# Expert outputs written in token order by indirect transfers, and small reorderings on GpSimd, ScalarE and VectorE in the attention layers of a two-layer decoder

## The reference, cut to what matters

```python
x = x + _L0_attn_ref(_layernorm(x), ...)          # 16 heads of 8
x = x + _L0_xattn_ref(_layernorm(x), ctx, ctx, ...)  # 16 heads of 8
x = x + _L0_ffn_ref(_layernorm(x), ...)           # 8 experts, top 2, F=512
x = x + _L1_attn_ref(_layernorm(x), ...)          # 16 heads of 64, rotary positions
x = x + _L1_xattn_ref(_layernorm(x), ctx, ctx, mask)
x = x + _L1_ffn_ref(_layernorm(x), ...)           # fake-quantised gated part
...
# _L0_ffn_ref
logits = jnp.einsum('bth,eh->bte', x, router_w) + router_b
topv, topi = jax.lax.top_k(logits, TOP_K)
gates = jax.nn.softmax(topv, axis=-1)
# per expert e: w = sum(gates * (topi == e)); y = (silu(x gw) * (x uw)) dw; acc + y * w
```

## Time and profile before

| | us |
|---|---|
| median of 3 runs | 1352.48 |
| lowest and highest run | 1347.32 to 1356.64 |
| profiled execution, its own time | 1356.87 |
| its span in the trace | 1355.1 |
| busy in the span: PE, DVE, POOL, ACT | 1055.9, 892.3, 548.8, 553.0 |
| granted TensorE clock, mean | 0.84 of full |

### The profile page before, as it was taken

One profiled execution on the slowest core, in us unless ns is written; L12 is line 12 of the kernel. 1 busy time (PEld: TensorE's weight loads), 2 busy tenths in 40 slices (PEclk: granted clock), 3 DMA queues, 4 the chain that ended last, 5 costly groups with the idle time before them and its releaser, 6 DMA issues. The chain is left out here.

```text
span 1355.1 us, 39532 instructions
## 1 busy us (share of the span) xinstructions
PE 1055.9 (78%) x14827; PEld 849.9 (63%) x14828; DVE 892.3 (66%) x2134; ACT 553.0 (41%) x877; POOL 548.8 (41%) x686
## 2 busy tenths in 40 slices
PE   2889895888967389999993899999999997462353
PEld 1466563555646289999992778788788786341012
DVE  2577663678762663444444689889889885546777
ACT  1456452555631015666651344444444443111343
POOL 3132313334402023333314878888888864203000
PEclk9799895899975559999996899999999999555555
DMA  3000001000024001111112000000000000111002
GB/s 83 1 2 0 1 1 32 17 9 15 2 84 166 8 14 42 47 48 46 46 36 84 16 13 10 12 10 10 12 10 11 10 0 19 46 48 31 0 0 62
DMA packets 33367, 37.54 MB, mean 28 GB/s; under 512 B 6344, under 2 KB 26507, under 8 KB 32908
## 3 DMA queue, kind: packets, MB, share of 16 engines
q1 hardware_dynamic: 28942, 27.64, 6.7%
q0 software_dynamic: 4352, 8.92, 2.5%
HBM read 27.63 MB, written 8.91 MB: 27 GB/s over the span
## 5 line engine op out<-in xcount | busy, mean ns | idle before, releaser
L1167 POOL DMA_INDIRECT e_x<-xn_rows,e_where x72 | 68.3, 948 | 205.4 <-DVE e_where L1148 119.1
L1137 DVE COPY e_y<-e_Y_ps 128x128 f32<-128x128 f32 x72 | 21.0, 292 | 110.9 <-PE e_Y_ps L1104 110.9
L1094 PE MATMUL e_G_ps<-e_xT,e_gate_here 128*128 128x128 f32 x576 | 78.3, 280 | 0.5 <-ACT e_up_here L1057 0.5
L1094 PE MATMUL e_U_ps<-e_xT,e_up_here 128*128 128x128 f32 x576 | 77.8, 279 | 0.0
L1104 PE MATMUL e_Y_ps<-m_down_w,e_hT 128*128 x576 | 76.3, 275 | 1.2 <-issue 1.0
L1303 POOL TENSOR_TENSOR a_RQ<-a_PQ 128x256 f32<-128x256 f32 x64 | 46.3, 724 | 75.4 <-DVE a_PQ L1648 75.4
L1572 ACT ACTIVATE a_OT<-a_VQ_ps 128x512 f32<-128x512 f32 x64 | 38.2, 597 | 89.0 <-PE a_VQ_ps L1468 89.0
L1056 ACT ACTIVATE e_gate_here<-m_gate_w 128x512 f32 x72 | 45.4, 630 | 70.3 <-PEq L85 44.9
L1094 PEld LDWEIGHTS e_G_ps<-e_xT,e_gate_here 128*128 128x128 f32 x576 | 72.0, 196 | 0.7 <-ACT e_up_here L1057 0.7
L1094 PEld LDWEIGHTS e_U_ps<-e_xT,e_up_here 128*128 128x128 f32 x576 | 71.8, 196 | 0.0
L1104 PEld LDWEIGHTS e_Y_ps<-m_down_w,e_hT 128*128 128x128 f32 x576 | 70.3, 192 | 0.9 <-issue 0.9
(11 more groups left out here) (302 smaller groups left out, 2885.5 us busy)
## 6 DMA issues: line engine op xcount, KB each, us to landing
slot_out<-e_y SPq DMA_DIRECT2D x72, 64.0 KB
x_ctxT<-in_ctxT SPq DMA_DIRECT2D x16, 256.0 KB
m_gate_w<-in_L_ffn_gate_w SPq DMA_DIRECT2D x1, 2048.0 KB
m_up_w<-in_L_ffn_up_w SPq DMA_DIRECT2D x1, 2048.0 KB
m_down_w<-in_L_ffn_down_w SPq DMA_DIRECT2D x1, 2048.0 KB
xn_rows<-r_xn SPq DMA_DIRECT2D x8, 256.0 KB
x_ctxK<-in_ctxK SPq DMA_DIRECT2D x8, 256.0 KB
out_x<-q_y SPq DMA_DIRECT2D x8, 256.0 KB, 2.2
```

The costliest lines, as they stand in the source:

```text
L1094: mm = nc.tensor.matmul(out[:, c * P:(c + 1) * P], w[:, p, c * P:(c + 1) * P], xT[:, p, :], start=True, stop=True)
L1167: nc.gpsimd.indirect_dma_start(out=x[:, j, :], out_offset=None, in_=k.xn_rows, in_offset=bass.IndirectOffsetOnAxis(ap=where[:, j, :], axis ...
```

## The change

Four things are changed. (1) The expert phase no longer stores its tiles to `slot_out`. The plan phase numbers the pairs 1 + choice*4096 + token, keeps these numbers per row as `targets` (0 for padding), and derives `tokens` from them by four more small instructions on DVE. POOL then writes each tile's rows by an indirect transfer to the row of `chosen_out` that `targets` names; padding rows all go to row 0. So that two of these transfers are never under way at once, POOL waits for the one before to have landed. `y` has four buffers, and the store of tile t stands on POOL behind the gather of tile t+8. (2) The wide attention reads both choices of a block by two plain transfers from SP, 128 KB each; POOL's gathers and ACT's index copies are gone. (3) In the wide attention combine moves from items 1 and 2 to items 0 and 1, statistics from item 3 to item 2, and power, centre and normalise from item 0 to item 3 of the step before. (4) In the narrow attention spread_k stands ahead of power.

```diff
@narrow_attention_phase, POOL
             def step(blk, p, prev, nxt):
+                if nxt:
+                    spread_k(blk + 1, 1 - p)
                 if nxt == 2:
                     power(blk + 2)
-                if nxt:
-                    spread_k(blk + 1, 1 - p)
                 add_bias(blk)
@plan_phase, DVE
-            nc.vector.tensor_copy(tokens[:], token_ps[:, 0:NT])
+            chained(nc.vector.tensor_copy(token_f[:], token_ps[:, 0:NT]))
+            nc.vector.tensor_copy(targets[:], token_f[:])
+            chained(ts(second[:], token_f[:], float(NU * P + 1), float(-NU * P), ALU.is_ge, ALU.mult))
+            chained(tt(token_f[:], token_f[:], second[:], ALU.add))
+            nc.vector.tensor_scalar(tokens[:], token_f[:], -1.0, 0.0, ALU.add, ALU.max)
@expert_phase, SP: the whole block is removed
-                wait_here(sp, y_ready, t + 1, passed)
-                sp.dma_start(k.slot_out[bass.ds(t * P, P), :], y[:, p, :]).then_inc(stored[p], 16)
@expert_phase, DVE
-            def output(t, p):
+            def output(t, j):
+                s = j % YB
+                if later(t, YB):
+                    dve.wait_ge(stored[s], (t // YB) * 16)
+                nc.vector.tensor_copy(target[:, s, :], targets[:, bass.ds(t, 1)])
                 dve.wait_ge(y_done, t + 1)
-                if later(t, 2):
-                    dve.wait_ge(stored[p], (t // 2) * 16)
-                nc.vector.tensor_copy(y[:, p, :], Y_ps[p][:, 0:C]).then_inc(y_ready, 1)
+                nc.vector.tensor_copy(y[:, s, :], Y_ps[j % 2][:, 0:C]).then_inc(y_ready, 1)
@expert_phase, POOL
+            def scatter(t, j):
+                s = j % YB
+                if later(t, 1):
+                    pool.wait_ge(stored[(j - 1) % YB], (t // YB + (1 if s else 0)) * 16)
+                wait_here(pool, y_ready, t + 1, passed)
+                nc.gpsimd.indirect_dma_start(
+                    out=k.chosen_out, out_offset=bass.IndirectOffsetOnAxis(ap=target[:, s, :], axis=0),
+                    in_=y[:, s, :], in_offset=None).then_inc(stored[s], 16)
+            def body(t, j, left):
+                gather(t, j)
+                if later(t, Q):
+                    scatter(t - Q, j)
@wide_attention_phase, SP
+            def load_chosen(nb, p):
+                if later(nb, 2):
+                    wait_here(sp, combined, (nb - 1) * 2, passed)
+                for i in range(2):
+                    rows = k.chosen_out[bass.ds(nb * TOK + (i * NU * P + 1), TOK), :].rearrange("(u t) c -> t u c", t=P)
+                    sp.dma_start(expert_rows[:, p, i], rows).then_inc(got[p], 16)
+            def prologue():
+                load_chosen(0, 0)
...  # then the seven weight loads as before, load_chosen(1, 1), load_chosen(2, 0)
@wide_attention_phase, POOL
             def step(blk, p, prev, nxt):
                 for g in range(G):
-                    if nxt and g == 0:
-                        power(blk + 1)
+                    if later(nxt, 2) and g == 3:
+                        power(blk + 2)
...
-                    if nxt == 3:
-                        gather(blk + 3, g, 1 - p)
@wide_attention_phase, ACT and DVE: normalise and centres alike
-                    if nxt and g == 0:
-                        normalise(blk + 1)
+                    if later(nxt, 2) and g == 3:
+                        normalise(blk + 2)
@wide_attention_phase, DVE
                     if later(nxt, 2):
-                        if g in (1, 2):
-                            combine(blk + 2, g - 1, p)
-                        if g == 3:
+                        if g in (0, 1):
+                            combine(blk + 2, g, p)
+                        if g == 2:
                             statistics(blk + 2)
```

More of the change, by code:

```diff
@@ L1020, in expert_phase @@
         y_ready = sem("y_ready")
-        stored = [sem("stored0"), sem("stored1")]
+        stored = [sem(f"stored{i}") for i in range(YB)]
         passed = sem("passed")
@@ L1036, in tiles @@
                 body(NT - Q + j, j, Q - j)
-        @block.sync
-        def _(sp):
-            def body(t, j, left):
-                p = j % 2
-                wait_here(sp, y_ready, t + 1, passed)
-                sp.dma_start(k.slot_out[bass.ds(t * P, P), :], y[:, p, :]).then_inc(stored[p], 16)
-            tiles(sp, body)
-            for q in stored:
-                sp.wait_ge(q, NT // 2 * 16)
         @block.scalar
@@ L1169, in body @@
                     in_offset=bass.IndirectOffsetOnAxis(ap=where[:, j, :], axis=0)).then_inc(x_in[j], 16)
-            tiles(pool, body)
+            def scatter(t, j):
[10 more added lines that the diff above has]
+                    scatter(t - Q, j)
+            for j in range(2 * Q):
+                body(j, j % Q, NT)
+            with pool.Fori(2, NT // Q) as i:
+                for j in range(Q):
+                    body(i * Q + j, j, NT)
+            for j in range(Q):
+                scatter(NT - Q + j, j)
+            for s in range(YB):
+                pool.wait_ge(stored[s], NT // YB * 16)
 def wide_attention_phase(nc, k):
@@ L1355, in prologue @@
                 rotate_k(0, 1)
+                power(1)
                 rotate_q(0, 2)
```

77 lines of the change are left out of this document (32 added, 45 removed).

## The result

| | before | changed |
|---|---|---|
| median of 6 runs, us | 1356.2 | 1344.62 |
| lowest to highest | 1347.32 to 1356.64 | 1343.56 to 1348.29 |
| profiled execution: time, span | 1356.87, 1355.1 | 1343.56, 1341.6 |

The ratio of the times is 0.9934, with a 95% interval of 0.9909 to 0.9959: the change gains 0.7%. I had forecast 1324, 32 us less than before's median of these six runs (28 less than the median known then). The sign was right and the size was not, and three of its terms were far off, one of them against the other two.

What follows compares the result with a forecast made beforehand. It took PE to bound the expert phase, and waits between engines the wide attention. Terms -14, +0.8, +15, -4, -4, -22.5 sum to -28.7: 1324 us for a median run, 1328 profiled; forecast's range 1315 to 1335, with rivals 1303 to 1347.

Steps and rivals of the forecast that it cites:

- Narrow attention, -14 forecast: Narrow attention: spread_k ahead of power ends PE's wait; 14 steps gain 1.0 us each, bounds 0 and -27.6.
- Plan phase, +0.8 forecast: Plan phase: four more small DVE instructions, hidden by nothing, cost 0.8 us, between 0.5 and 1.5.
- Expert phase, +15 forecast: Expert phase: the chain of indirect stores, each waiting for the last to land, sets its end; +15 us, bounds +1.7 and +40.
- Chained, that is 2.15 + 0.81 = 2.96 us from store to store: Expert phase: landing 2.15 us, taken from a gather, plus 0.81 to start again; 0.17 more than PE's 2.79 a tile.
- rival 2: Expert phase: store chain takes over; landing time L from 2.55 us eats the gain, L 3.0 gives 1385 us; chance 0.12.
- Start of the wide attention, -4 forecast: Wide attention's start: plain loads replace eight gathers, so PE starts at about 723.2 instead of 727.22; -4 us.
- The first two blocks, -6.6 forecast: Wide attention: block 0 gains 4 us without gathers ahead of power, the next block, of 26.15 us, gains 2.6.
- Steady blocks, -20 forecast: Wide attention: twelve blocks go from 25.16 to 23.5 us, 1.66 each, with gathers gone and chores moved ahead.
- the trace holds its own experiment, 23.78 us: Wide attention: a block without gathers but with combine, statistics and late power took 23.78 us, bounding the new block time.
- Rival 3: Wide attention: DVE is next to limit, blocks stay at 24.2 us, gain 13 instead of 22.5, 1334 us; chance 0.12.
- Rival 1: Expert phase: stores keep PE's pace, landing within 1.98 us; cost 1.7 instead of 15, 1311 us; chance 0.25.
- rival 4: Narrow attention: the edit does nothing because another wait comes last; 1338 us; chance 0.06.

Runs made afterwards that it cites:

- experiment 4: Changed kernel with each padding row sent to a row of its own and POOL's wait for the store before removed: 1347.1 us, ratio 0.9946.
- 7: Kernel before with spread_k first, plus one indirect POOL store per expert tile that nothing in the phase waits for, plain output stores kept: 1379.01 us, ratio 1.0201.
- experiment 6: Kernel before with spread_k first, plus a second indirect gather per expert tile into an unread buffer, plain stores kept: 1314.23 us, ratio 0.977.
- experiment 2: Changed kernel with the wide attention's combine, statistics, power, centre and normalise back in their old items, plain loads kept: 1340.78 us, ratio 0.9886.

## Why the prediction was off, point by point

- **Narrow attention, -14 forecast, -38 measured.** The mechanism was right (the wait for KX gone, the row maximum directly behind xn, power covered), the size was not, in two ways. The step "1.0 us a step, xn should take 1.51" took xn's length as given; but POOL's spread_k ran beside it, and without it xn takes 1.10. Where the clock stood at 1.00, the steps from residual to residual went from 20.3 to 18.8 us in self attention and from 20.0 to 18.6 in cross attention: 14 steps by 1.4 to 1.5 are 20 us, an estimate. The other 18 lie where PE's clock had been at half: 0.93 and 0.86 of full before, 0.99 and 0.92 after. A block from 158.0 to 182.5 took 24.5 us at a mean clock of 0.79, the one before it 20.15 at 1.00, and two steps of cross attention at 0.92 took 21.0 and 20.9. The sum had no term for it, and even the lower bound (-27.6) missed. Why there are fewer such stretches was not tried; that PE waits less is the nearest reading. (`KT` is ready 10.0 us ahead of xn in the rows shown, not 11, which changes nothing.)
- **Plan phase, +0.8 forecast, +0.84 measured:** from DVE's read of `token_ps` to the expert phase's first index copy it is 0.97 us before (496.34 to 497.31) and 1.81 now (458.13 to 459.94). Router, plan and the start of the expert phase together took 117.2 instead of 117.6 us, for other reasons.
- **Expert phase, +15 forecast, +44.5 measured** from the first y copy to the first instruction of the next phase (199.8 us before, 244.3 now). That the chain of stores sets the end was right. The step of the prediction that failed is "Chained, that is 2.15 + 0.81 = 2.96 us from store to store". From first to last store it is 235.2 us for a forecast of 71 x 2.96 = 210.2: 57 steps of 3.16 are 11 us of that (2.25 to land and 0.91 to start again, each 0.1 over the forecast), and 14 longer ones 14 us (the last four tiles with all rows to one row, tiles at an expert's end, one of 5.59). For the repeated rows the sum had no term, though rival 2 named them. The other 4.5 us lie behind the last store's start, since POOL is now the last to finish: of the 7.90 us to the next phase, the landing is some 3.1. That 2.15 came so near the store's 2.25 was luck. It was the end of the gather's packets, which I took for its landing: the last semaphore event of the gather at 598.01 came 2.48 us after its start, and with that the same sum gives steps of 3.29 and an expert phase some 39 us longer (an estimate), near the measured one for a wrong reason.
- **Not in the sum:** I held the chain to be the only price of indirect stores. Experiments 4 and 7 show that without a chain they cost as much, by late hand-overs from PE. The row that I reasoned from, the gather, is harmless (experiment 6).
- **The Trainium skill's rule on DRAM** (page "DMA: Bandwidth & Descriptors", section "Anatomy of one DMA — SWDGE (gpsimd) path") did not decide: chained, the store into DRAM stepped 0.19 us faster than the gather into SBUF. **The Trainium skill's rule on the shared port** (page "SBUF — State Buffer", section "SBUF: two separate sides") shows in no store: POOL takes 985 ns to issue one in the kernel and 961 where DVE does nothing, and they land after 2.25 us in both.
- **Start of the wide attention, -4 forecast:** from the phase's first instruction to the first transposes 13.86 us before (713.36 to 727.22) and 10.01 after: -3.9. As forecast, the weights are now what comes last: ACT has normalised at 726.71, and PE starts at 729.49, when the last weight load has landed. **The first two blocks, -6.6 forecast:** 53.3 became 47.1. Both right.
- **Steady blocks, -20 forecast, -6.7 measured** (24.60 for 25.15, twelve times). Step that failed: "the trace holds its own experiment, 23.78 us". I measured that block between POOL's power instructions, and the second of them stood 2.34 us ahead of PE's transposes where the first stood 2.05 ahead, no gather preceding it. Between PE's transposes the same block takes 1106.47 - 1082.39 = 24.08, and with gathers gone and the old places it is 24.3 (experiment 2). And the move that I took for a help cost 0.3 a block: centre at the head of item 3 waits for power (0.64 us), ACT's normalise stands before V, and PE waits for V 0.5 us a block.
- **Rivals.** Rival 2, the stores take over, came nearest: the average step of 3.31 corresponds to its L of 2.5, just under the point of 2.55 from which it eats the gain, though a landing took 2.25 and the rest came from the repeated rows and the slower start. Rival 3 was true as well, for another reason (not DVE, but the chain moved into item 3). Rival 1 and rival 4 were wrong. The three errors, -24, +29 and +13, leave 18; the rest of the kernel gained 3 and router and plan 1 that I had not counted on, which is 14 of the 15 us by which the sum missed the profiled execution (1328 against 1343.56). That it missed by no more is luck: the first error cancels more than half of the other two.

## What to carry to other kernels

Price an operation that the trace doesn't hold by a kernel of its own before you price a change by it: the landing was within 0.1 us of what I had read off its nearest relative, but by luck, and neither the start behind the waits, nor the repeated rows, nor the disturbance of other engines could be read off it. Take a landing from the last semaphore event and not from the last packets, which ended 0.3 us earlier here. If you take a block's period from a trace, take it between two instructions of the engine that sets it. And when a large change gains little, time its parts one by one: here one call moved ahead of another was worth 38 us, and the rewrite around it cost 27.

## What the runs showed of the hardware that I had not expected

- Beside POOL's unchained indirect stores, PE's signals to DVE and ACT came late. With one store per tile a tile took 3.39 us instead of 2.74, and 147 of 277 of PE's semaphore events came 0.3 to 3 us behind the end of their instruction. In experiment 4 a y copy started 2.8 us behind the end of PE's product, together with an ACT instruction that waited for a later product. Two gathers per tile, or a plain POOL store, did not do it (2.74 us both). With chained stores one trace had the delays and another of the same phase had not. The mechanism is not shown.
- An indirect store with repeated rows lands later: 0.32 us for 64 rows to one, 0.86 for 128; a gather of one row 128 times steps in 3.88 instead of 2.71.
- The same DVE instructions on SBUF (xn) took 1.10 us alone, 1.51 beside spread_k on POOL and 2.46 beside the end of spread_k and the bias addition.
- A store landed 2.25 us after its start, and the next began 0.27 us later with the wait on the transfer itself (steps of 2.52 us), 0.83 later with two waits and a count as instructions of their own in front of it (3.06). The kernels differ in more than that, and it was not tried by itself.
- A gather's last semaphore event came 2.5 us after its start, 0.3 us behind the end of its last packets.
